# Projection of the attended values in split fp32r passes instead of fp32 matmuls

## What is computed

```
x = x + tanh(g_xattn[0]) * cross_attention_0(layernorm(x), ctx)     # one head, 154 keys
x = x + tanh(g_ffn[0])   * sum over 8 experts of (silu(h @ Wg) * (h @ Wu)) @ Wd
x = x + tanh(g_xattn[1]) * cross_attention_1(layernorm(x), ctx)     # 8 heads of 64, below
x = x + tanh(g_ffn[1])   * routed_experts(layernorm(x))             # top 1 of 8, capacity 256
```

```
xn  = layernorm(x) * gamma + beta
q   = xn @ Wq * 64 ** -0.5;  k, v = split(ctx @ Wkv)
out = softmax(q k^T, masked) v      # for each of 8 heads
x  += tanh(g) * (out @ Wout)        # Wout is 512 x 256
```

## Time and profile before

| | us |
|---|---|
| median of 3 runs (lowest, highest) | 1296.63 (1294.59, 1300.03) |
| the profiled execution | 1291.54 |
| its span | 1289.8 |
| TensorE busy in the span | 1243.7 |
| VectorE busy | 919.9 |
| ScalarE busy | 635.9 |
| GpSimd busy | 550.4 |

### The profile page before, as it was taken

How to read it: one execution, slowest core, us unless ns; L and a number is a source line. 1 busy time by engine, 2 the same in 40 slices (tenths; PEclk the granted TensorE clock), 3 DMA queues, 4 the chain that set the end, 5 groups by cost and what they waited for, 6 DMA issues and landing times.

```text
span 1289.8 us, 17755 instructions
## 1 busy us (share of the span) xinstructions
PE 1243.7 (96%) x6212; PEld 1010.4 (78%) x6212; DVE 919.9 (71%) x1667; ACT 635.9 (49%) x1348; POOL 550.4 (43%) x542
## 2 busy tenths in 40 slices
PE   7999999999999999999999999999999989999995
PEld 5778888888888888888888888888888877777774
DVE  5987777777776777777777777777767675777655
ACT  2455554544555554545555555445555535535543
POOL 3635654444444444444444444444444024343434
PEclk9999999999999999999999999999999998999998
DMA  4100300000000001100000000000000220000022
GB/s 134 50 1 1 116 25 25 25 25 25 25 25 25 25 25 41 34 25 25 25 25 25 25 25 25 26 25 25 25 25 1 68 96 1 18 34 2 34 71 91
DMA packets 41672, 44.21 MB, mean 34 GB/s; under 512 B 4140, under 2 KB 40048, under 8 KB 41455
## 3 DMA queue, kind: packets, MB, share of 16 engines
q1 hardware_dynamic: 37984, 38.87, 9.2%
q0 software_dynamic: 1488, 3.57, 0.8%
q10 hardware_dynamic: 2111, 0.63, 0.2%
HBM read 35.27 MB, written 8.32 MB: 34 GB/s over the span
## 4 chain that ended last, share of the span: by engine, by line
PE 85%; DVE 6%; ACT 3%; POOL 2%; issue 2%; DMA 1%; ACTq 0%; POOLq 0%; DVEq 0%
PE bank L1060 25%; PE bank L1059 25%; PE bank L1061 25%; PE bank L1265 2%; ACT PC L829 2%; PE bank L1274 1%; PE bank L1249 1%; DVE nmC L1724 1%; POOL out_dram L646 1%; DVE xnC L1486 1%; PE bank L1225 1%; PE bank L1286 0%; POOL rstd L488 0%; PE bank L1021 0%; PE bank L965 0%
## 5 line engine op out<-in xcount | busy, mean ns | idle before, releaser
L1059 PE MATMUL bank<-xop_hi,w_hi 128*128 128x512 f32 x896 | 351.2, 392 | 1.7 <-ACT half_g L760 1.2
L1060 PE MATMUL bank<-xop_lo,w_hi 128*128 128x512 f32 x896 | 351.9, 393 | 0.0
L1061 PE MATMUL bank<-xop_hi,w_lo 128*128 128x512 f32 x896 | 351.1, 392 | 0.0
L1664 DVE TENSOR_TENSOR acc<-bank,acc 128x512 f32<-128x512 f32 x248 | 170.8, 689 | 119.9 <-PE bank L1061 119.6
L1650 DVE TENSOR_TENSOR hid_lo<-hid,hid_hi 128x512 fp32r<-128x512 f32 x256 | 213.7, 856 | 34.6 <-ACT hid_hi L783 34.5
L1059 PE MATMUL bank<-hid_hi,wd_hi 128*128 128x512 f32 x512 | 202.5, 395 | 0.6 <-DVE hid_lo L1650 0.6
L1060 PE MATMUL bank<-hid_lo,wd_hi 128*128 128x512 f32 x512 | 203.0, 397 | 0.0
L1059 PEld LDWEIGHTS bank<-xop_hi,w_hi 128*128 128x128 f32 x896 | 168.5, 188 | 42.7 <-ACT half_g L760 1.5
L1061 PE MATMUL bank<-hid_hi,wd_lo 128*128 128x512 f32 x512 | 201.4, 393 | 0.0
L1060 PEld LDWEIGHTS bank<-xop_lo,w_hi 128*128 128x128 f32 x896 | 168.4, 188 | 38.4
L1061 PEld LDWEIGHTS bank<-xop_hi,w_lo 128*128 128x128 f32 x896 | 168.3, 188 | 37.4
(11 more groups left out here) (216 smaller groups left out, 1775.2 us busy)
## 6 DMA issues: line engine op xcount, KB each, us to landing
raw_gu<-in_L_ffn_Wg_dram SPq DMA_DIRECT2D x32, 256.0 KB, 2.7
raw_gu<-in_L_ffn_Wu_dram SPq DMA_DIRECT2D x32, 256.0 KB, 3.2
raw_d<-in_L_ffn_Wd_dram SPq DMA_DIRECT2D x32, 256.0 KB, 3.6
slots<-empty_row SPq DMA_DIRECT2D x1, 2080.0 KB, 10.8
xr<-slots SPq DMA_DIRECT2D x8, 260.0 KB, 5.3
x_res<-in_x_dram SPq DMA_DIRECT2D x4, 512.0 KB, 5.1
we_raw<-in_L_ffn_W_dram SPq DMA_DIRECT2D x8, 256.0 KB, 4.5
out_dram<-x_res SPq DMA_DIRECT2D x3, 512.0 KB, 2.9
```

The lines of the kernel that those rows point to most:

```text
L1059: mm(ps, w, a, start=start, stop=False, skip_group_check=True)
L1060: mm(ps, w, a_low, start=False, stop=False, skip_group_check=True)
L1061: return mm(ps, w_low, a, start=False, stop=True, skip_group_check=True)
L1664: nc.vector.tensor_tensor(out=to, in0=ps, in1=to, op=ALU.add).then_inc(acc_added, 1)
```

## The change

`oT` becomes a pair: ScalarE rounds bank 5 to fp32r (`oT_hi`, the new `o_hi_out`), VectorE then writes bank 5 minus `oT_hi` (`oT_lo`, in `o_out`). `Wouts` becomes a pair as well, split once by GpSimd (`split_out_weights`) ahead of its first chunk; `Wout_lo` is written over `Wouts`. `project` issues twelve fp32r matmuls of 128x256 instead of four fp32 ones: eight with `oT_hi`, then, behind the wait for `oT_lo`, four with `oT_lo`. `o_hi_out(c, j)` stands in ScalarE's queue behind pT_out(j, 2), ahead of `x_rows` and `route_exp`. The semaphore `c_prep_ps` is folded into `prep_pe` with an offset of 10.

```diff
@@ -130,6 +130,7 @@
     PREP_DVE = 6
+    PREP_PE = 10
 
@@ -264,10 +265,13 @@
         xn4T = sk.take("xn4T", [P, KB, CH], F32)
-        Wouts = sk.take("Wouts", [P, HB, D], F32)
+        Wouts = Arena(nc, sk.at, raw_at).take("Wouts", [P, HB, D], F32)
+        Wout_lo = sk.take("Wout_lo", [P, HB, D], F32R)
+        oT_lo = sk.take("oT_lo", [P, HB, P], F32R)
 
         weT = sg.take("weT", [P, E, KB, D], F32)
+        Wout_hi = sg.take("Wout_hi", [P, HB, D], F32R)
         Wq_hi = sg.take("Wq_hi", [P, KB, INNER], F32R)
@@ -289,7 +293,7 @@
         rdenC = [sd.take(f"rdenC{i}", [P, HEADS], F32) for i in range(2)]
-        oT = sd.take("oT", [P, HB, P], F32)
+        oT_hi = sd.take("oT_hi", [P, HB, P], F32R)
 
@@ -327,12 +331,12 @@
         c_v = sem("c_v")
-        c_prep_ps, c_prep_act = sem("c_prep_ps"), sem("c_prep_act")
+        c_prep_act = sem("c_prep_act")
         c_yT_ps, c_ln, c_xnT_ps, c_xnT, c_xn_lo, c_q_ps, c_q_act, c_q_dve, c_x2 = (
             sem(n) for n in ("c_yT_ps", "c_ln", "c_xnT_ps", "c_xnT", "c_xn_lo", "c_q_ps", "c_q_act", "c_q_dve", "c_x2"))
-        c_sim_ps, c_nmax, c_probs, c_rden, c_norm, c_pT_ps, c_pT_act, c_pT_dve, c_o_ps, c_o, c_out_ps, c_res = (
+        c_sim_ps, c_nmax, c_probs, c_rden, c_norm, c_pT_ps, c_pT_act, c_pT_dve, c_o_ps, c_o_hi, c_o, c_out_ps, c_res = (
             sem(n) for n in ("c_sim_ps", "c_nmax", "c_probs", "c_rden", "c_norm", "c_pT_ps", "c_pT_act", "c_pT_dve",
-                             "c_o_ps", "c_o", "c_out_ps", "c_res"))
+                             "c_o_ps", "c_o_hi", "c_o", "c_out_ps", "c_res"))
         r_ln, r_xnT_ps, r_xnT, r_logit_ps, r_shift, r_exp, r_one, r_loc_ps, r_loc_read, r_x, r_slot, scattered = (
@@ -591,6 +595,14 @@
                                             oob_is_err=False).then_inc(scattered, 16)
+
+            def split_out_weights():
+
+                pool.wait_ge(wout_in, 16)
+                nc.gpsimd.tensor_copy(Wout_hi[:], Wouts[:]).then_inc(consts_ready, 1)
+                pool.wait_ge(consts_ready, 7)
+                nc.gpsimd.tensor_tensor(out=Wout_lo[:], in0=Wouts[:], in1=Wout_hi[:].bitcast(F32),
+                                        op=ALU.subtract).then_inc(consts_ready, 1)
 
@@ -632,6 +644,7 @@
             keep_own_heads(1)
+            split_out_weights()
             chunk(0, front=True, route=False)
@@ -853,6 +866,10 @@
 
+            def o_hi_out(c, j):
+                act.wait_ge(c_o_ps, c * CT + j + 1)
+                nc.scalar.copy(oT_hi[:].rearrange("p k t -> p (k t)"), bank[5][:]).then_inc(c_o_hi, 1)
+
             def chunk(c, front, route):
@@ -862,12 +879,14 @@
                     pT_out(c, j, 2)
+                    o_hi_out(c, j)
                     if route and j == 0:
                 pT_out(c, CT - 1, 2)
+                o_hi_out(c, CT - 1)
                 if front:
...
@@ -1268,10 +1287,16 @@
                 t = c * CT + j
+                pe.wait_ge(c_o_hi, t + 1)
+                wait_if(pe, c_res, t)
+                if t == 0:
+                    pe.wait_ge(consts_ready, 8)
+                for k in range(HB):
+                    mm(bank[7][:, 0:D], oT_hi[:, k, :], Wout_hi[:, k, :], start=k == 0, stop=False, skip_group_check=True)
+                    mm(bank[7][:, 0:D], oT_hi[:, k, :], Wout_lo[:, k, :], start=False, stop=False, skip_group_check=True)
                 pe.wait_ge(c_o, t + 1)
-                wait_if(pe, c_res, t)
                 for k in range(HB):
-                    ins = mm(bank[7][:, 0:D], oT[:, k, :], Wouts[:, k, :], start=k == 0, stop=k == HB - 1)
+                    ins = mm(bank[7][:, 0:D], oT_lo[:, k, :], Wout_hi[:, k, :], start=False, stop=k == HB - 1, skip_group_check=True)
                 ins.then_inc(c_out_ps, 1)
...
@@ -1737,8 +1762,9 @@
             def o_out(c, j):
-                dve.wait_ge(c_o_ps, c * CT + j + 1)
-                nc.vector.tensor_copy(oT[:].rearrange("p k t -> p (k t)"), bank[5][:]).then_inc(c_o, 1)
+                dve.wait_ge(c_o_hi, c * CT + j + 1)
+                nc.vector.tensor_tensor(out=oT_lo[:].rearrange("p k t -> p (k t)"), in0=bank[5][:],
+                                        in1=oT_hi[:].rearrange("p k t -> p (k t)").bitcast(F32), op=ALU.subtract).then_inc(c_o, 1)
 
...

```

More of the change, by code:

```diff
@@ L883, in value_out @@
             def value_out(b, g):
-                act.wait_ge(c_prep_ps, HB + 3 * b + g + 1)
+                act.wait_ge(prep_pe, PREP_PE + HB + 3 * b + g + 1)
                 of = P_BLOCKS[g]
@@ L889, in _ @@
             for m in range(0, HB, 2):
-                act.wait_ge(c_prep_ps, m + 1)
+                act.wait_ge(prep_pe, PREP_PE + m + 1)
                 nc.scalar.copy(k1T[:, m, :], bank[m][:, 0:AK]).then_inc(c_prep_act, 1)
@@ L1190, in _ @@
                     ins = mm(bank[m][:, 0:AK], Wkvs[:, k, m * P:(m + 1) * P], ctxT[:, k, :], start=k == 0, stop=k == KB - 1)
-                ins.then_inc(c_prep_ps, 1)
+                ins.then_inc(prep_pe, 1)
             def queries(f):
@@ L1933, in key_out @@
             def key_out(m):
-                dve.wait_ge(c_prep_ps, m + 1)
+                dve.wait_ge(prep_pe, PREP_PE + m + 1)
                 nc.vector.tensor_copy(k1T[:, m, :], bank[m][:, 0:AK]).then_inc(prep_dve, 1)
```

## The result

The changed kernel took 1308.8 us (median of four runs, 1307.89 to 1309.90); the kernel before took 1295.6 beside it. The ratio is 1.0101, with a 95% interval of 1.0083 to 1.0119. Run again on another chip beside the experiments it gave 1.0105 [1.0083, 1.0128]. So the change costs 13 us (11 to 15 by the first interval). I had forecast 3.3, and a range that ended at 1306.

A forecast was written before the change was run, and what follows sets the result against it. TensorE bounds the first chunk and tile 0 of the others, VectorE tile 1 of chunks 1 to 3. 3.7 us lost there less 0.4 gained in the first chunk gives +3.3 on 1296.63: 1299.9 us, range 1293 to 1306.

The forecast's parts named there:

- Projection: TensorE's twelve passes at 0.117 us take 1.40 us instead of 1.80, saving 0.40 a tile.
- First chunk: Chunk without route: maxes 0.26 us later, TensorE 0.40 earlier at each tile; 0.4 us gained, bounds 0 and 1.6.
- Chunks 1 to 3, the queue: At tile 1 ScalarE's new copy delays route_exp, so the maxes of tile 3 start 1.63 us later, three times.
- E: The end of an attention; the maxes of tile 3 were forecast at E + 4.03, before at E + 2.40.
- GpSimd's split: One cast and one subtraction, 1.04 and 2.35 us, hidden before GpSimd's first normalisation with about 2 to spare.
- The subtraction beside GpSimd: VectorE's new subtraction, with one input in PSUM, never waits for GpSimd; priced at 0.60 us.
- Tiles 2 and 3 nothing: In the chunks with route, the projections of tiles 2 and 3 were counted as gaining nothing.
- TensorE gets more idle time, not more work: Behind the late maxes of chunks 1 to 3 everything moves along; 1.63 - 0.40 = 1.23 us a chunk.
- the rival: TensorE's clock falls in the new gap: 1.1 to 1.6 us in each of three chunks, 1303.2 to 1304.7; 14%.
- The clock leaving 1.00 in these chunks: Named sign of being wrong: TensorE's granted clock leaves 1.00 in the chunks with route.

The follow-up runs named there:

- e10: The changed kernel, unedited, run again on another chip: 1304.4 us, 1.0105 of the kernel before.
- e9: The changed kernel with four further unused passes behind each projection: 1302.6 us, 1.0090 of the kernel before.
- e8: e1 with the route choice behind the maxes of tile 3 and the location matmuls behind tile 2's attention: 1295.1 us, 1.0011 of the kernel before.
- e7: e1 with four further unused passes behind each projection: 1292.7 us, 0.9995 of the kernel before.
- e1: The changed kernel with ScalarE's route exponential put back ahead of the rounding copy at tile 1: 1296.3 us, 1.0006 of the kernel before.
- e2: The kernel before, with ScalarE made to wait for tile 1's attention ahead of the route exponential: 1302.3 us, 1.0055 of the kernel before.
- e4: The changed kernel with the rounding copy moved from ScalarE to VectorE, ahead of the subtraction: 1305.4 us, 1.0068 of the kernel before.

## Why the prediction was wrong

Two full chunks side by side settle it. The stretches run from the attention of tile 1 in chunk 2 to that of tile 2, of tile 3, of the next chunk's tile 0, and its tile 1 (columns as in the earlier trace rows). The kernel before:

```profile
1175.64:1184.62 8.98, 8.54 (x84) 7.04 (x83) 7.02 (x25) 4.03 (x20) 2.43 (x2) 1.00 0.01 2
1184.62:1190.53 5.91, 5.37 (x53) 4.54 (x52) 5.60 (x20) 0.89 (x3) 1.86 (x2) 1.00 0.01 3
1190.53:1210.54 20.01, 17.49 (x138) 13.82 (x137) 12.55 (x38) 10.80 (x37) 11.25 (x11) 1.00 0.16 54
1210.54:1219.61 9.07, 8.56 (x86) 7.25 (x85) 3.61 (x11) 5.89 (x25) 3.04 (x3) 1.00 0.00 0
```

The changed kernel, in the profile of e10:

```profile
1178.80:1189.97 11.17, 8.80 (x88) 7.51 (x87) 6.50 (x26) 4.92 (x21) 2.63 (x3) 0.95 0.00 0
1189.97:1197.43 7.46, 7.46 (x58) 6.89 (x57) 4.86 (x18) 1.17 (x2) 1.01 (x1) 0.62 0.01 2
1197.43:1217.80 20.37, 17.37 (x142) 13.66 (x141) 13.04 (x39) 11.39 (x38) 11.88 (x11) 1.00 0.15 53
1217.80:1226.56 8.76, 8.25 (x90) 7.19 (x89) 3.43 (x11) 6.43 (x26) 3.03 (x3) 1.00 0.01 2
```

The forecast for this chunk was 1.23 us more; it grew by 47.76 - 43.97 = 3.79. Of these 1.92 are the attention of tile 2 (4.16 against 2.24). From the last transposes to that attention it is 1.94 us (from 1188.03) against 1.40 in e9 at the upper level (1142.57 to 1143.97), which is 0.54. What is left, 1.33, is the delay at full clock.

- **Projection**: right. 1.40 us and 0.117 a pass forecast; 0.12 and 1.51, with 0.11 in the first pass behind an idle time.
- **First chunk**: right. 0.4 forecast; from its first attention to the next chunk's 39.79 us (e10) against 40.16, 0.37.
- **Chunks 1 to 3, the queue**: right in its place and its size. E + 4.05. The first stretch grew by 2.19, less the 0.54 that is 1.65, for maxes later by 1.63 in the forecast; tile 0 gave back 0.31 where I had 0.40. At full clock that is 1.33 a chunk against 1.23 forecast. 3 x 1.33 - 0.37 = 3.6 against the sum of 3.3, and the level over all of e10's runs is 3.8 above before's.
- **GpSimd's split**: right. 1.04 and 2.37 us, and idle time of 2.17 left behind them, where I counted about 2.
- **The subtraction beside GpSimd**: right. It took 0.68 to 0.69 us in all 16 tiles of both profiles, in four of them beside GpSimd's `rstd<-ve,mhalf`, which ran for 0.9 to 1.0 us.
- **Tiles 2 and 3 nothing**: right for the forecast's purpose; the stretches from tile 2 to tile 0 differ by 0 in sum once the 1.92 is taken off (27.83 - 1.92 against 25.92).
- **"TensorE gets more idle time, not more work"**: this is the step that failed. I let idle time cost only itself. It cost the clock as well: 1.92 + 0.54 = 2.46 us in this chunk and about as much in the two others, 7.4 in all, where the rival said 1.1 to 1.6 for each, and it came in every one of six chunks profiled, where I gave it 14%. The clock leaving 1.00 in these chunks was the sign of being wrong that I had named. From the first attention to the last e10 took 164.42 us and before 152.03, 12.4 more: 3.6 of delay, 7.4 of these falls, and one more fall ahead of tile 1 in chunk 1 (10.33 us in place of 8.76, 1.6) make 12.6. By the runs: 27.6 us more at the lower clock at 0.35 are 9.7, and with the level's 3.8 that makes 13.5 against 13.0 measured.

Two readings misled me. Against the rival I held that the other chunks were idle for 3.3 of 44 us and still held 1.00; that counts idle time over a chunk, but what changed is one piece of it, 0.44 us before and 1.69 after, with another of 0.66 just ahead. And I priced the fall by ten transposes, although behind the new gap stood an attention of 34 matmuls, all of which ran at the lower level.

What brings the clock down at tile 2 has two parts. Here are the versions whose gap at tile 2 was not filled on purpose (e8, with its other order, is left out), by the maxes' start and by TensorE's idle pieces between the attentions of tiles 1 and 2, which are the same in all chunks of a kernel to 0.02 us:

| | maxes of tile 3 | idle pieces, us | tile 2 slow |
|---|---|---|---|
| before | E + 2.40 | 0.44 | 0 of 3 |
| e7 | E + 2.4 | 0.50 | 0 of 3 |
| e1 | E + 2.4 | 0.98 | 1 of 3 |
| e2 | E + 3.55 | 1.12, 0.44 | 0 of 3 |
| e9 | E + 4.04 | 0.66, 1.23 | 0 of 3 |
| e4 | E + 3.1 | 1.49 | 3 of 3 |
| the change (two profiles) | E + 4.05 | 0.66, 1.69 | 6 of 6 |

Late maxes with a projection of the old length (e2, e9) did not do it; late maxes with the short one (e4, the change) did each time. The short one alone (e1) did it once, so it is not harmless either. The sum of the idle pieces does not sort the versions: e9 has 1.89 us and none fell, e4 1.49 and all fell. The longest single piece does, but for e1. The prediction had noted both parts, as a delay of 1.63 and a gain of 0.40, and set them against each other; for the clock they pull the same way.

The Trainium skill describes another kernel in "TensorE: Matmul & The Clock Gate", § A second HAM failure mode, where short idle times between groups of matmuls let the clock go to and fro, and the matmuls' median duration does not show it. The traces here agree, on a mixed stream: the median of the 544 attention matmuls is 273 ns before and after, and only the longest ones differ, 325 and 476 ns. It takes the rows in order of time to see the fall.

Still open: why the clock falls at a given chunk start in one run and not in another (the kernel before spent 18 to 42 us at the lower clock, from run to run), by how much each such fall was the change's, and why e1, with the same 0.98 us of idle time in three chunks, lost the clock in one. The count of chunks rests on one profile for each kernel, two for the change.

## What to carry to other kernels

A new wait on a busy TensorE has two prices, the delay and the clock of what stands behind it; look up whether the engine has just had a short stream or a long one, and what long work comes next, before calling the clock safe. Making a stream on TensorE shorter between waits is no gain by itself: here 0.40 us a projection were saved, and as much unused work put back cost nothing that could be measured. And when a helper is added to an engine's queue, walk the queue: a copy that waits for TensorE must not stand ahead of an instruction that others wait for.

## What the runs showed of the hardware

- A us at the lower clock went with 0.35 us more of the kernel's time (199 runs), not the 0.5 that half the clock would cost a stream that waits for nothing. That the rest is hidden behind other engines' work is likely, but was not tested. Even the kernel before spends 23 to 31 us of a run there in the median, and its scatter of up to 8 us on one chip follows it (0.38 us for a us over its own 61 runs on the first two chips, with a level for each chip).
- A 128x256 fp32r pass costs 0.12 us from start to start at the upper level and 0.21 at the lower (1178.21 to 1178.42 in the changed kernel, chunk 2):

```profile
1177.99 0.41 PE L1295 MATMUL bank<-Wout_hi,oT_hi 128*128 128x256 f32 x1
1178.21 0.41 PE L1296 MATMUL bank<-Wout_lo,oT_hi 128*128 128x256 f32 x1
1178.42 0.41 PE L1295 MATMUL bank<-Wout_hi,oT_hi 128*128 128x256 f32 x1
```
